# A two-layer decoder: experts' weights fetched and turned during the router, and the experts' steps in one sequence across chunks

## Time and profile before

| | us |
|---|---|
| three timed runs | 7079.01, 7087.08, 7086.99; median 7086.99 |
| span of the profiled execution (first to last instruction) | 7062.9 |
| median less span (what lies around the instructions) | 24.1 |
| router and experts of layer 0 (f0r, f0e), start of loads to the last add to X | 2627.7 to 3131.7 |
| feed-forward part (de) | 5099.6 to 5202.4 |
| router and experts of layer 1 (f1r, f1e) | 6720.8 to 7052.0 |

### The profile page before, as it was taken

The page is one execution under the profiler, slowest core; times in us unless marked ns, Lnnn a source line. Parts: engine busy times, 40 slices in busy tenths (PEclk is TensorE's granted clock), DMA queues, the critical chain, the costliest instruction groups (busy, mean ns, idle before and its releaser), DMA issues. The chain is left out here.

```text
span 7062.9 us, 139442 instructions
## 1 busy us (share of the span) xinstructions
PE 5536.5 (78%) x46679; PEld 2990.7 (42%) x46679; DVE 4746.6 (67%) x8810; ACT 3148.0 (45%) x4716; POOL 2122.0 (30%) x2723
## 2 busy tenths in 40 slices
PE   3686647688888865978498999996567699999759
PEld 2343425222222232434256888885525233333234
DVE  5464663699999954456656777763453699999644
ACT  0233424467767741223433444442214477777522
POOL 0101324467767740003026555542204100000000
PEclk6898978799999977989796888876778799999879
DMA  2220015322222210002243434331115322222200
GB/s 61 47 48 10 7 27 182 107 56 57 58 57 59 57 43 19 0 0 100 104 138 111 120 111 122 110 100 60 49 30 191 100 62 66 64 64 66 56 12 12
DMA packets 747531, 484.44 MB, mean 69 GB/s; under 512 B 516504, under 2 KB 682240, under 8 KB 741568
## 3 DMA queue, kind: packets, MB, share of 16 engines
q1 hardware_dynamic: 747200, 480.04, 24.0%
HBM read 282.34 MB, written 196.37 MB: 68 GB/s over the span
## 5 line engine op out<-in xcount | busy, mean ns | idle before, releaser
L1481 ACT ACTIVATE c0a_raised<-c0a_sb 128x1024 f32<-128x1024 f32 (+1 forms) x832 | 836.5, 1025 | 321.7 <-PE c0a_sb L1293 317.4
L1246 POOL TENSOR_SCALAR c0a_prob<-c0a_raised 128x1024 f32<-128x1024 f32 (+1 forms) x832 | 864.7, 1039 | 382.3 <-ACT c0a_raised L1481 349.2
L1481 ACT ACTIVATE c1a_prob<-c1a_sb 128x1024 f32<-128x1024 f32 (+1 forms) x832 | 828.5, 1029 | 204.5 <-PE c1a_sb L1293 200.7
L1369 DVE TENSOR_REDUCE c0a_pmax<-c0a_sa 128x2 f32<-128x802 f32 (+1 forms) x704 | 697.1, 990 | 68.9 <-PE c0a_sa L1261 64.6
L1369 DVE TENSOR_REDUCE c1a_pmax<-c1a_sa 128x2 f32<-128x802 f32 (+1 forms) x704 | 698.3, 992 | 66.2 <-PE c1a_sa L1261 62.1
L1261 PE MATMUL c0a_sa<-c0a_K,c0a_Q 48*128 48x401 bf16 (+1 forms) x2048 | 475.1, 351 | 188.2 <-DVE c0a_pmax L1369 104.5
L1261 PE MATMUL c1a_sa<-c1a_K,c1a_Q 48*128 48x401 bf16 (+1 forms) x2048 | 465.5, 345 | 104.5 <-DVE c1a_pmax L1369 49.6
L1312 PE MATMUL c0a_pv<-c0a_prob,c0a_V 128*9 128x256 f32 x6656 | 530.9, 390 | 4.7 <-POOL c0a_prob L1246 4.1
L1312 PE MATMUL c1a_pv<-c1a_prob,c1a_V 128*9 128x256 f32 x6656 | 518.0, 382 | 0.7 <-issue 0.5
L1261 PEld LDWEIGHTS c0a_sa<-c0a_K,c0a_Q 48*128 48x128 bf16 x2048 | 130.0, 94 | 678.3 <-DVE c0a_pmax L1369 335.1
L2997 PE MATMUL dd_lb<-dd_src 64*128 64x128 f32 (+1 forms) x3584 | 360.4, 348 | 37.7 <-POOL dd_src L2980 15.2
(11 more groups left out here) (608 smaller groups left out, 11310.3 us busy)
## 6 DMA issues: line engine op xcount, KB each, us to landing
dd_src<-unit_in SPq DMA_DIRECT2D x32, 1024.0 KB, 7.8
k_ctx<-c0k_parts SPq DMA_DIRECT2D x16, 1200.8 KB, 4.7
c0a_K<-k_ctx SPq DMA_DIRECT2D x128, 150.1 KB
k_ctx<-c1k_parts SPq DMA_DIRECT2D x16, 1200.8 KB, 4.7
c1a_K<-k_ctx SPq DMA_DIRECT2D x128, 150.1 KB
unit_in<-ds_raw SPq DMA_DIRECT2D x32, 512.0 KB, 2.6
unit_v<-ds_vs SPq DMA_DIRECT2D x32, 512.0 KB, 2.6
unit_in<-dp_res SPq DMA_DIRECT2D x32, 512.0 KB, 2.9
```

What stands on the lines that cost most here:

```text
L1246: pool.tensor_scalar(prob[0:r, in_ring(v, c), :, :, :], raised[0:r, in_ring(v, c), :, :, :], 1.0, math.exp(-FLOOR), ALU.min, ALU.max).then ...
L1369: dve.tensor_reduce(pmax[:, u, :, 2 * pr + s, k], sa2[:, :, 0:w], AX.X, ALU.max).then_inc(a_reduced, 1)
L1481: act.activation(dst[0:r, in_ring(v, c), :, :, :], sb_[0:r, in_both(v, c), :, :, :], ACT.Exp).then_inc(b_exp, 1)
```

```diff
@@ router_stage
+                for m, lo, hi, source in sources:
+                    sp.dma_start(nat[:, m, lo:hi, :].rearrange("p s (e i) -> p (s e) i", i=source.shape[2]),
+                                 source).then_inc(fetched, 16)
...
+                pool.memset(pick[:, :, :], 0.0).then_inc(pick_built, 1)
...
                 router_scores(pe, XT, gw, logits, E).then_inc(scored, 1)
+                pe.wait_ge(fetched, 16 * len(sources))
+                for i in range(NW):
+                    q = i // 4
+                    if i % 4 == 0 and q >= 2:
+                        pe.wait_ge(e_copied, q - 1)
+                    m, s = divmod(i, S)
+                    ins = pe.transpose(wp[:, q % 2, (i % 4) * P:(i % 4 + 1) * P], nat[:, m, s, :], ident[:, :])
...
                 pe.wait_ge(w_ready, 1)
...
                     act.activation(other[:, :, :], choice[:, :, :], ACT.Exp).then_inc(squashed, 1)
+                for q in range(-(-NW // 4)):
+                    m = min(4, NW - 4 * q)
+                    act.wait_ge(e_turned, q + 1)
+                    act.activation(wT[:, :, :, :].rearrange("p m s f -> p (m s f)")[:, q * 512:q * 512 + m * P],
+                                   wp[:, q % 2, 0:m * P], ACT.Copy).then_inc(e_copied, 1)
@@ experts_stage
+                def down(k):
+                    n, s = divmod(k, S)
+                    if s == 0 and n >= 1:
+                        pe.wait_ge(oT_ready, n)
+                    pe.wait_ge(hid_ready, k + 1)
+                    pe.matmul(op[:, :], wT[:, 2, s, :], hid[:, k % 2, :], start=(s == 0), stop=(s == S - 1)
+                              ).then_inc(downed, 1)
...
-                over(pe, CHUNKS, chunk)
+                if fetched is not None:
+                    pe.wait_ge(fetched, 16 * fetches)
+                for k in range(STEPS):
+                    n, s = divmod(k, S)
+                    gate_up(k)
+                    if s == 2 and n >= 1:
+                        turn_out(n - 1)
+                    if k >= 1:
+                        down(k - 1)
+                down(STEPS - 1)
                 turn_out(CHUNKS - 1)
...
+                for k in range(STEPS):
+                    n, s = divmod(k, S)
+                    act.wait_ge(g_ready, k + 1)
+                    if k >= 2:
+                        act.wait_ge(hu_ready, k - 1)
+                    act.activation(sg[:, k % 2, :], gp[:, k % 2, :], ACT.Silu).then_inc(sg_ready, 1)
+                    if s == 0 and n >= 1:
+                        copy_out(n - 1)
+                copy_out(CHUNKS - 1)
@@ gate_stage
+                for m, source in [(0, t["L1_attn_w_ff1"].rearrange("h (s f) -> h s f", f=P)),
+                                  (1, t["L1_attn_w_ff3"].rearrange("h (s f) -> h s f", f=P)),
+                                  (2, t["L1_attn_w_ff2"].rearrange("(s f) h -> f s h", f=P))]:
+                    sp.dma_start(ff[:, m, :, :], source).then_inc(ff_fetched, 16)
                 over_pairs(sp, TILES, unit)
```

More of the change, by code:

```diff
@@ L1904, in router_stage @@
             keep = st.sb("keep", [E, NT])
+        S = wT.shape[2]
+        NW = 3 * S
+        routed = pick.shape[1]
+        nat = st.sb("nat", [P, 3, S, P])
         logits = st.ps("logits", T)
+        wp = st.ps("wp", [P, 2, 512])
         tp = st.ps("tp", [P, 4, 512])
@@ L1941, in _ @@
                     pool.memset(grest[:, :], 1.0).then_inc(built, 1)
+                pool.memset(pick[:, :, :], 0.0).then_inc(pick_built, 1)
+                pv = pick[:, :, :].rearrange("p s (a i) -> p s a i", a=per)
+                for b in range(3):
+                    pool.wait_ge(pick_built, b + 1)
+                    pool.affine_select(out=pv, in_=pv, compare_op=ALU.not_equal, fill=1.0, base=-32 * b,
+                                       pattern=[[-per, routed], [-1, per], [0, P // per]],
+                                       channel_multiplier=1).then_inc(pick_built, 1)
             @block.tensor
@@ L2080, in rank_of, with experts_stage @@
     link(dve.tensor_reduce(rank[:, :, :], more[:, :, :, :], AX.X, ALU.add))
[L2083 to L2087 removed]
+def experts_stage(nc, name, X, XT, ident, GS, wT, pick, fetched=None, fetches=0):
+    S = wT.shape[2]
     C = 512
     CHUNKS = NT // C
+    STEPS = CHUNKS * S
+    routed = pick.shape[1] if pick is not None else 0
     with Stage(nc, name) as st:
[L2091 to L2094, removed]
         sg = st.sb("sg", [P, 2, C])
@@ L2117, in experts_stage, with routed_up_to @@
         added = st.sem("added")
-        NW = 3 * S
+        def routed_up_to(k):
+            n, s = divmod(k, S)
+            return n * routed + min(s + 1, routed)
         with st.block() as block:
[L2121 to L2140, removed]
@@ L2153, in _, with gate_up @@
[L2153 to L2161, removed]
+                def gate_up(k):
+                    n, s = divmod(k, S)
+                    x = XT[:, n * C:(n + 1) * C]
+                    if k >= 2:
+                        pe.wait_ge(sg_ready, k - 1)
+                        pe.wait_ge(hu_ready, k - 1)
+                        pe.wait_ge(hid_ready, k - 1)
+                    pe.matmul(gp[:, k % 2, :], wT[:, 0, s, :], x, start=True, stop=True).then_inc(g_ready, 1)
+                    pe.matmul(up[:, k % 2, :], wT[:, 1, s, :], x, start=True, stop=True).then_inc(u_ready, 1)
+                    if s < routed:
+                        pe.matmul(wp[:, k % 2, :], pick[:, s, :], GS[:, n * C:(n + 1) * C], start=True, stop=True
+                                  ).then_inc(r_ready, 1)
@@ L2195, in _, with copy_out @@
             def _(act):
[L2196 to L2207, removed]
+                def copy_out(n):
                     act.wait_ge(downed, (n + 1) * S)
-                    if not early(n, 1):
+                    if n >= 1:
                         act.wait_ge(o_turned, n)
                     act.activation(oT[:, :], op[:, :], ACT.Copy).then_inc(oT_ready, 1)
-                over(act, CHUNKS, chunk)
+                for k in range(STEPS):
+                    n, s = divmod(k, S)
+                    act.wait_ge(g_ready, k + 1)
+                    if k >= 2:
+                        act.wait_ge(hu_ready, k - 1)
[3 more added lines that the diff above has]
+                copy_out(CHUNKS - 1)
             @block.vector
@@ L2217, in add_out @@
                     dve.wait_ge(o_turned, n + 1)
-                    xs = X[:, bass.ds(n * 4, 4), :]
+                    xs = X[:, n * 4:(n + 1) * 4, :]
                     dve.tensor_tensor(xs, xs, tp[:, :].rearrange("p (k d) -> p k d", k=4), ALU.add).then_inc(added, 1)
[L2221 to L2239, removed]
@@ L2240, in _ @@
-                over(dve, CHUNKS, chunk)
+                for k in range(STEPS):
+                    n, s = divmod(k, S)
+                    dve.wait_ge(sg_ready, k + 1)
+                    dve.wait_ge(u_ready, k + 1)
+                    if k >= 2:
+                        dve.wait_ge(hid_ready, k - 1)
+                    dve.tensor_tensor(hu[:, k % 2, :], sg[:, k % 2, :], up[:, k % 2, :], ALU.mult).then_inc(hu_ready, 1)
+                    dve.wait_ge(hu_ready, k + 1)
+                    if k >= 2:
+                        dve.wait_ge(downed, k - 1)
+                    if s < routed:
+                        dve.wait_ge(r_ready, routed_up_to(k))
+                        ins = dve.tensor_tensor(hid[:, k % 2, :], hu[:, k % 2, :], wp[:, k % 2, :], ALU.mult)
+                    else:
+                        ins = dve.tensor_copy(hid[:, k % 2, :], hu[:, k % 2, :])
+                    ins.then_inc(hid_ready, 1)
+                    if s == 3 and n >= 1:
+                        add_out(n - 1)
```

75 lines of the change are left out of this document (39 added, 36 removed).

## The result

| | before | after |
|---|---|---|
| median of 11 runs each, us | 7077.36 | 7099.82 |
| lowest and highest run | 7054.66 to 7087.08 | 7090.95 to 7120.70 |
| span of the profiled execution | 7062.9 | 7114.2 |

The account below looks back on a forecast made before the run. No engine is busy all the time; PE idles at stage heads, then bounds the stage except at chunk ends. Savings 34.4 + 20.3 + 7.1 + 14.7 = 76.5 us make the span 6986.4; plus 24.1, 7010 us, range 6999 to 7030.

Parts of the forecast that it names:

- Heads: Starts of f0e, f1e and de, where PE makes no product: 34.4, 20.3 and 7.1 us saved.
- The cover in the router: Layer 0's router: PE's 33.5 us wait hides the rest of the fetch and the turning, at cost 0.
- the harmless place of the loads in the gate stage: Three de loads ahead of the first load of `o` in SP's list: cost 0.
- the clock: Start of each mixture: 1.2 GHz for 4.5 or 3.4 us, costing 2.1 us each, 4.2 together.
- Chunk ends: f0e, f1e, de: the last down product no longer waits for `hid`; 21 x 0.70 = 14.7 us saved.
- Loop written out: ... I take 0: Edited stages: some six chunks more of straight code for PE, ACT and DVE in each, cost 0.
- straight code is not supplied in time: Rival, three edited stages: each chunk's code costs an unhidden 2.0 us load, 36 us come back, 7046; 6%.
- The 24.1 that the median has over the span: Whole kernel: 24.1 us added to the forecast span of 6986.4 to give the median, 7010.5.
- The chance of 2% for slower: Rival, router: the fetch lands after the choice, at 2755 in layer 0, making the kernel slower by 0.2%; 2%.
- theory A: Post-result theory, c1a's loop: added code moved its start, so it touches eight 16,384-byte pieces, not seven; eight are not held.

Follow-up runs that it names:

- p1: Kernel before with only the moved weight fetches, turns and copies, experts' old loop kept, no filler: median 7008.29 us, ratio 0.9928 to before.
- p2: Kernel before with only the steps written out in the new sequence, plus 32 one-column matmuls in c1n: median 7055.52 us, ratio 0.9988 to before.
- p3: Kernel before with only the experts' chunk loop written out, plus 32 one-column matmuls in c1n: median 7064.10 us, ratio 1.0001 to before.

## Why the prediction failed, step by step

- **Heads: right.** 34.4, 20.3 and 7.1 forecast; 34.3, 19.7 and 6.3 in p1. The cover in the router and the harmless place of the loads in the gate stage were as read. So was the clock: 0.50 over f0e's first 4.4 us; the 0.61 and 0.62 at the heads of f1e and de in after are, by an estimate from these means, 3.3 and 3.4 us at the lower level, near the shorter of the two stretches forecast (in p1 de had 0.50 over 4.5 us).
- **Chunk ends: right**, 13.7 in p2 against 14.7, so 0.65 for each in place of 0.70.
- **"Loop written out: ... I take 0" is the step that failed.** I asked only whether the written-out stages get their code in time. They do (p3), and ds was a fair witness for that. What I did not ask is what the added instructions do to code behind them. They move the start of c1a's loop by 127 places, from seven pieces to eight, and this costs 112.9 us in a stage that the change doesn't touch.
- **The rival "straight code is not supplied in time" had the right resource and the wrong place and price.** I put 36 us on it, in three stages; there it is 0. I rested it on two held lines of code for an engine, and on that reading c1a's loop could never have been held. The section of the Trainium skill that I cited ("Advanced Engine Details and Errata", section "ISA Cache") also gives TensorE 128 KB of code memory, with 16 KB to a line, and I passed over this. Here a loop over seven pieces ran 13 passes without a packet, so two is wrong for TensorE. The Trainium skill has a statement that would have served ("Runtime: NRT & Kernel Launch", section "Instruction fetch mechanics"): TensorE's code memory is 128 KiB, filled first in, first out in blocks of 16 KiB, which is eight of them (a note under it speaks of two again). The runs at both ends agree: seven pieces and the next one fetched ahead make eight, and stay; eight and the next make nine, and nine packets come in each pass (117 / 13). The passes without a packet at 70 and 102 are not explained by this alone. That the soft edge follows from when the ninth is asked for is a guess that no run tested.
- **"The 24.1 that the median has over the span" was wrong as a part of the sum.** The profiled run of after took 7116.26 with a span of 7114.2, so 2.1 lie around it. The rest of the 24.1 was spread between runs, of which c0a's chance is a large part. The same saving taken from the median of 11 runs gives 7001.
- **The chance of 2% for slower** came from rivals in the edited stages alone. Nothing in it stood for stages that only lie behind them.

## What to carry to other kernels

When an edit adds or removes instructions of an engine, count them ahead of each long loop that comes later, and work out how many 16,384-byte pieces the loop then touches. For TensorE a loop over seven was held, and one that reached 100 instructions and more into an eighth was not, which was worth 8.5 us for each pass of 68; in between it was fetched again in some passes. The border itself had to be found by runs: the count from the compiled program is off from it by an unknown amount. If an unedited stage slows down, look at the row of the instruction queue in that stage before anything else: packets within a held loop should be none, and a few one-column products in an idle place move the loop back at no cost that was seen here. To compare two versions of a kernel fairly, put the loops of both at held places first.

## What the runs showed of the hardware that I had not expected

- TensorE kept the code of a loop of 1670 instructions, with no packet in 884 us (before), where by theory A it touches seven pieces. At places 165 and 166 it fetched nine packets in each pass, and in c0a, at place 62, 0 to 6 of 13 passes were hit, differently from one profile to the next.
- Around two pauses of 3.0 and 1.6 us the granted clock was 0.56 over 4.9 us and 0.77 over 13 more; c1a's mean falls from 0.98 to 0.91, and PE's busy time rises from 1042 to 1101 us for the same 12,096 products. That is half of the loss.
- A small load behind large ones can hold SP for long: 7.14 us for one of 64 KB behind the three of 1 MB in the router. The next two, of the same size and form, held it 0.43 us each, so it was not the load itself; what SP waited for is not shown. It cost nothing here, as PE was busy with the scores until 2666.
